# A gated delta rule on one Trainium2 core: the state's update by two products of 64 stationary columns, one per head

## The reference, cut to what matters

```
def step(S, inp):
    q_t, k_t, v_t, g_t, b_t = inp
    S = S * jnp.exp(g_t)[..., None, None]
    mem = jnp.einsum('bhk,bhkv->bhv', k_t, S)
    delta = (v_t - mem) * b_t[..., None]
    S = S + jnp.einsum('bhk,bhv->bhkv', k_t, delta)
    o_t = jnp.einsum('bhk,bhkv->bhv', q_t * scale, S)
    return (S, o_t)
```

## Time and profile before

| | us |
|---|---|
| median of 3 runs | 4779.81 |
| the three runs | 4772.99, 4779.81, 4781.04 |
| the profiled execution: its own time | 4777.68 |
| its span, first to last instruction | 4776.2 |
| TensorE busy | 4666.4 (98%) |
| VectorE busy | 4140.4 (87%) |
| ScalarE busy | 3397.6 (71%) |
| GpSimd busy | 3153.8 (66%) |

### The profile page before, as it was taken

The page is one execution under the profiler, slowest core; times in us unless marked ns, Lnnn a source line. Parts: engine busy times, 40 slices in busy tenths (PEclk is TensorE's granted clock), DMA queues, the critical chain, the costliest instruction groups (busy, mean ns, idle before and its releaser), DMA issues. The chain is left out here.

```text
span 4776.2 us, 140986 instructions
## 1 busy us (share of the span) xinstructions
PE 4666.4 (98%) x44336; PEld 3735.3 (78%) x44336; DVE 4140.4 (87%) x9914; ACT 3397.6 (71%) x10287; POOL 3153.8 (66%) x4511
## 2 busy tenths in 40 slices
PE   6999999999999999999999999999999999999797
PEld 4788888888888888888888888888888888888565
DVE  6888888888888888888888888888888889998576
ACT  5777777777777777777777777777777777777443
POOL 5666666666666666666666666666666667777565
PEclk9999999999999999999999999999999999999899
DMA  5111111111111111111111111111111111211010
GB/s 179 48 33 44 33 53 35 41 43 41 46 33 44 33 53 33 44 36 48 46 33 44 33 52 33 44 33 50 40 39 43 34 53 42 61 46 44 20 40 32
DMA packets 206732, 212.94 MB, mean 45 GB/s; under 512 B 17218, under 2 KB 180180, under 8 KB 206036
## 3 DMA queue, kind: packets, MB, share of 16 engines
q1 hardware_dynamic: 206036, 204.06, 13.8%
HBM read 186.31 MB, written 17.70 MB: 43 GB/s over the span
## 5 line engine op out<-in xcount | busy, mean ns | idle before, releaser
L1015 DVE SCALAR_TENSOR_TENSOR cv<-ps_a,wqkv,cv 128x511 f32<-128x511 f32 (+2 forms) x1536 | 1145.6, 746 | 182.1 <-ACT cv L1008 161.9
L1220 POOL TENSOR_TENSOR bm<-bat,mask 128x256 f16<-128x256 f32 x1536 | 1032.2, 693 | 0.6
L1000 PE MATMUL ps_a<-xin,wqkv 128*128 128x512 f32 x2048 | 1001.9, 612 | 3.0 <-PEq L109 1.5
L1270 ACT ACTIVATE m<-b 128x256 f16<-128x256 f32 x1536 | 596.7, 388 | 376.5 <-PE b L1265 376.4
L1008 ACT ACTIVATE cv<-ps_a,wqkv 128x512 f32<-128x512 f32 x512 | 352.2, 688 | 553.4 <-PE ps_a L1000 553.2
L1281 DVE TENSOR_TENSOR tt<-tt,b 128x256 f16<-128x256 f16 x1536 | 635.2, 414 | 116.0 <-PE b L1276 115.6
L1323 ACT CAST tt<-bu 128x256 f16<-128x256 f32 x1536 | 578.3, 376 | 1.0 <-PE b L1276 0.4
L1455 PE MATMUL ps_a<-wout,yT 128*128 128x256 f32 x2048 | 547.7, 390 | 0.5 <-ACT yT L1449 0.5
L1000 PEld LDWEIGHTS ps_a<-xin,wqkv 128*128 128x128 f32 x2048 | 349.7, 191 | 250.7 <-issue 250.7
L1148 PE MATMUL ps_b<-wgate,xin 128*128 128x256 f32 x2048 | 494.9, 384 | 0.2 <-DVE vtok L1171 0.2
L1197 DVE SCALAR_TENSOR_TENSOR bat<-ps_a,w,dec 128x256 f32<-128x256 f32 x1024 | 435.5, 477 | 40.4 <-DVE w L1067 22.6
(11 more groups left out here) (258 smaller groups left out, 12232.4 us busy)
## 6 DMA issues: line engine op xcount, KB each, us to landing
xin<-xT_scratch SPq DMA_DIRECT2D x128, 512.0 KB, 4.0
grow<-g_scratch SPq DMA_DIRECT2D x256, 256.0 KB, 4.6
gam<-g_scratch SPq DMA_DIRECT2D x256, 96.0 KB, 2.8
n_x<-in_x SPq DMA_DIRECT2D x16, 512.0 KB, 4.1
xT_scratch<-acc SPq DMA_DIRECT2D x16, 512.0 KB, 4.9
out_y<-e_yo SPq DMA_DIRECT2D x16, 512.0 KB, 2.6
gate_tok<-in_x SPq DMA_DIRECT2D x56, 128.0 KB, 2.9
wqkv<-in_w_qkv SPq DMA_DIRECT2D x32, 128.0 KB, 3.1
```

The source lines that it names most:

```text
L1000: ins = pe.matmul(ps[:], wqkv[:, k, j * P:(j + 1) * P], xin[p][:, k, :], start=k == 0, stop=k == KT - 1)
L1015: s.done(dve.scalar_tensor_tensor(y[:, r:], ps[:, 0:T - r], tap[:, j, TAPS - 1 - r:TAPS - r], y[:, r:], ALU.mult, ALU.add), f"a_tap{j}{r}")
L1220: s.done(pool.tensor_tensor(half_of(bm[:, l, units(g), :], l, 1), half_of(bt[:, units(g), :], l, 1), half_of(c["mask"][:, l, :].unsqueeze( ...
L1270: s.done(act.mul(half_of(m1[:, l, units(g), :], l, 0), half_bank(bank, l), -1.0), f"b_Me{l}{g}")
```

## The change

`ktok` loses its two zero blocks: it has two blocks of 64 per chunk, head 0 and head 1. `c_SU` takes 64 stationary columns per head; the product of head 0 goes to partitions 0 to 63 of `cs` and that of head 1 to partitions 64 to 127, both to columns 0 to 127. Each product still has all 128 rows and 128 moving columns. `c_S` becomes two instructions, one per head, each over 64 partitions x 128, on the diagonal block alone. The zero blocks of `state` are set once by VectorE before the loops. The two memsets of `ktok` on GpSimd go. `SLOT_ORDER` and all waits stay.

```diff
-    c["ktok"] = [sb(f"ktok{p}", [P, CH - 1, 4, DK]) for p in range(2)]
+    c["ktok"] = [sb(f"ktok{p}", [P, CH - 1, 2, DK]) for p in range(2)]
...
-        for p in range(2):
-            step(pool.memset(c["ktok"][p][:], 0.0))
             yield
...
-                    s.done(dve.tensor_tensor(ktok[p][:, :, 0:4:3, :],
+                    s.done(dve.tensor_tensor(ktok[p][:],
...
                             for h in range(2):
-                                ins = pe.matmul(cs[:, h * DV:(h + 1) * DV],
-                                                ktok[p][:, m, 2 * h:2 * h + 2, :].rearrange("p b e -> p (b e)"), uu[:, h, :],
+                                ins = pe.matmul(cs[h * DK:(h + 1) * DK, 0:DV], ktok[p][:, m, h, :], uu[:, h, :],
                                                 start=True, stop=True)
...
-                            new = cs[:, 0:2 * DV].rearrange("p (h e) -> p h e", h=2)
-                            if m == 0:
-                                ins = dve.tensor_copy(state[:], new)
-                            else:
-                                ins = dve.scalar_tensor_tensor(state[:], state[:], gend[p][:, m - 1:m], new, ALU.mult,
-                                                               ALU.add)
+                            for h in range(2):
+                                d = slice(h * DK, (h + 1) * DK)
+                                if m == 0:
+                                    ins = dve.tensor_copy(state[d, h, :], cs[d, 0:DV])
+                                else:
+                                    ins = dve.scalar_tensor_tensor(state[d, h, :], state[d, h, :], gend[p][d, m - 1:m],
+                                                                   cs[d, 0:DV], ALU.mult, ALU.add)
                             s.done(ins, f"c_S{m}")
...
+        dve.memset(state[:], 0.0)
         load_first()
```

More of the change, by code:

```diff
@@ L324, in build_later @@
             step(pool.tensor_copy(c["m1"][:, lev, 1:NU, :], c["m1"][:, lev, 0:1, :].broadcast_to([P, NU - 1, P])))
-            yield
-        for p in range(2):
-            step(pool.memset(c["ktok"][p][:], 0.0))
             yield
```

## The result

| | before | after |
|---|---|---|
| median of 4 runs each | 4779.03 us (4772.99 to 4781.04) | 4832.24 us (4828.72 to 4834.14) |
| ratio after/before, 95% interval | | 1.0113 (1.0102 to 1.0125) |
| profiled execution: time, span | | 4834.14, 4832.7 |

The kernel became 53 us slower, 0.42 us for each of the 128 iterations. The forecast was slower by 26 us (12 for TensorE and 14 for VectorE). The sign was right, TensorE's share was right, and the size in all was half of what came, since VectorE's share was three times as large.

The account below looks back on a forecast made before the run. The prediction took TensorE's own sequence as the bound. To the profiled 4777.7 us it added 12 for TensorE and 14 for VectorE, 4804, or 4806 us as a median against 4779.8; range 4786 to 4850.

Parts of the forecast that it names:

- TensorE's sequence is the bound: With all slots full, whatever lengthens or shortens TensorE's own sequence changes the kernel one for one; busy 3999.99 of 4000 us.
- In, inside and out of the 64 columns, +12 us: At `c_SU`: heads run side by side, but two array-shape switches per step eat the saving; +0.095 us per iteration, +12 us.
- the rival of 4845: At `c_SU`: passes keep strict program order, three places per step, +39 us on top of the forecast; chance 0.08.
- Two instructions at `c_y`'s price, +0.13 us, bounded by 0 and 0.2: At `c_S` on VectorE: two instructions cost 0.26 us each, as `c_y`'s do, against 0.39 for one; +0.13.
- Only `c_S1`'s delay counts, through `c_R2` to `c_Z2`, with 0.02 of room: Of the three state updates only this one delays TensorE, by 0.11 us per iteration, +14 us; the others are hidden.
- VectorE's part is hidden: Rival at `c_S`: the halves cost no more than the whole, so `c_R2` is not late; 4792 us, chance 0.15.
- the serial tiles: Rival at `c_SU`: the two column tiles do not run side by side, +81 us on top, 4887 us; chance 0.10.
- the free switch: Rival at `c_SU`: switching between 128 and 64 columns costs nothing, so the kernel gets faster, 4708 us; chance 0.05.
- The price behind the switch: Rival: `c_O`'s float32 loads behind `c_SU` hide, 2 x 0.10 less per iteration, and VectorE's part too; within 0.2%, chance 0.05.

Follow-up runs that it names:

- e1: Changed kernel, but the state's update stays one instruction over 128 partitions x 256, as before; 4793.93 us, ratio 1.0032 against the kernel before.
- e3: Kernel before, with the state's update in two instructions, each of all 128 partitions x 128 columns; 4789.94 us, ratio 1.0028.
- e4: Kernel before, with the state's update in two instructions of 64 partitions x 128, both on partitions 0 to 63; 4787.49 us, ratio 1.0024.
- e2: Kernel before, `c_SU` untouched, with the state's update in two instructions, lower and upper 64 partitions, x 128; 4817.86 us, ratio 1.0090.
- e7: Kernel before, with the state's update in two instructions of 64 partitions x 128, both on partitions 64 to 127; 4810.63 us, ratio 1.0073.
- e9: Changed kernel, with the upper half of the state's update ahead of the lower; 4816.05 us, ratio 1.0081 against the kernel before.
- e10: Changed kernel, with `c_acc0` moved behind `c_y1` in the order; 4801.24 us, ratio 1.0042 against the kernel before.
- e6: Changed kernel, with both heads' products on partitions 0 to 63, so on the same 64 array columns; 4907.72 us, ratio 1.0274 against before.
- e8: Kernel before, with `c_acc0` moved behind `c_R2` in the order; 4799.73 us, ratio 1.0055.

## Why the prediction was half right, point by point

*TensorE's sequence is the bound.* Right: 0.436 us more per iteration in it, x 128 = 56, is the whole of the 53 us.

*In, inside and out of the 64 columns, +12 us.* Right, term by term: 0.16, 0.007, 0.20 and 0.21 were measured as forecast, and e1 has 12.8 by its period. Passes in strict program order, the rival of 4845, are out for column tiles too: the starts are 0.007 apart in pairs. Two things about that rival were less certain than the prediction put them. That a product's passes are issued one behind the other is read from `c_O`, where L1386 stands twice and then L1387 twice; the records of a pair do not say which product they belong to. And its "does not agree" goes for passes alone. Taken for whole products, program order is not contradicted: the third product of `b_kk` signals its end on the seventh record and the fourth on the eighth, whose start is 0.006 us later.

*Two instructions at `c_y`'s price, +0.13 us, bounded by 0 and 0.2.* **This is the step that failed.** The term took both overlaps of 0.08 for granted, and the runs show that neither is there when the halves begin at different partitions. 0.13 is the price of a second instruction, and e3 and e4 have it. The split costs 0.35 (0.74 to 0.75 against 0.39), beyond the upper bound of 0.2. That bound counted two whole records, 2 x 342 - 480, but subtracted the length of a record of the one instruction. What that instruction costs is the distance to the next start, 0.39. With 0.39 the bound is 0.29; 0.045 us between ends of records and the held starts (0.014 and 0.031) and 0.01 of longer records (0.340 and 0.355) make the 0.35. The reason behind it is the row chosen: `c_y`'s two instructions both begin at partition 0, and so does every row. None of the rows it used has an instruction on partitions 64 to 127 between two that begin at partition 0, and the prediction took "64 partitions" for the open question, where it was the first partition.

The Trainium skill has the rule: the page "VectorE: DVE Perf Modes", section "Two Vector instructions with no wait between them", says, as a model, that an instruction whose input or output begins in another group of 32 partitions than the last one did is held until every earlier VectorE instruction has finished. The traces of e2, e3, e4, e7 and e9 agree in each case: 0.354 behind a record of 0.34 where it changes, 0.26 where it does not. The prediction did not weigh this rule. Worked from the rows of before, it would have given 2 x 0.342 - 0.39 - 0.02 = 0.27 per iteration, 35 us, and 4827 in all.

*Only `c_S1`'s delay counts, through `c_R2` to `c_Z2`, with 0.02 of room.* Right, and shown by TensorE's distances and by e10: (0.35 - 0.02) x 128 = 42, and 12 + 42 = 54 against 53. The delays behind the other two updates are hidden, as forecast; e1 and e2 leave 0.014 us per iteration over that no term explains.

*The rivals.* That VectorE's part is hidden is out (e2), and so are the serial tiles (e6), program order (the pairs), and the free switch (`c_SU` needs 0.16 + 0.20 beside the way in). The price behind the switch is not covered: `c_O` has 0.21.

## What to carry to other kernels

Price a split by a row that differs in the same way: number of instructions, shape, and where in the partitions each begins. On VectorE, put pieces that begin at the same partition next to each other, and let the change of the first partition fall into time in which the engine waits anyway. To lose little by such a split, look for the first instruction behind it that the bounding engine waits for, and move work that nobody waits for out from between them; but first see which hole that work fills (e8).

## What the runs showed of the hardware that was not expected

- Two VectorE instructions one behind the other overlap by about 0.08 us of their records when both begin at the same partition (0 and 0: 0.26 apart at 0.34 long; 64 and 64: 0.27 at 0.353). When the first partition changes they do not: 0.354 from 0 to 64 (record 0.340), 0.388 from 64 to 0 (record 0.355), 0.368 from 64 to 0 in e9 (record 0.353). Each change costs 0.09 to 0.13 us. Half the partitions cost as much as all (e4 0.53 us, e3 0.52).
- Two float32 products on two column tiles of 64 run fully side by side, 0.007 us apart, even when they write one PSUM bank; on one tile the same four matmuls take 0.21 us more (0.58 against 0.37).
- This gain is used up by the two changes of the array's shape: 0.095 us in and 0.092 out in the trace of after, 0.04 for the first load inside, which nothing covers, and 0.10 behind it, where the next product is float32.
